# Jobs of a two-layer transformer megakernel laid out anew: layer 0 as a written-out overlapping program, experts' scores from fp16 parts, two plain heads per strip of TensorE, and work moved to ScalarE and GpSimd

## The reference, cut to what matters

```python
x = ln(x + L0_attn(x))   # rms norm; k, v, r = x@W; scan s = ew*s + k*v; (sigmoid(r)*wkv)@Wo;
                         # then rms norm, 128->512 leaky relu, square, 512->128
x = ln(x + L0_ffn(x))    # 8 experts 128->256->128, top 2 of 8, run densely and weighted by the scores
x = ln(x + L1_attn(x))   # "plain" attention: 16 heads of 8, q and k rms-normed per head
x = ln(x + L1_ffn(x))    # 4 experts, each a whole 16-head attention over its own tokens, top 2 of 4
```

## Time and profile before

| | |
|---|---|
| median of 3 runs | 1957.21 us (1956.88 to 1971.77) |
| profiled execution, its own time | 1968.32 us |
| its span, first to last instruction | 1966.5 us |
| busy: TensorE / VectorE / ScalarE / GpSimd | 79% / 56% / 36% / 17% |
| mean granted TensorE clock | 0.828 |
| DMA over the span | 39.13 MB, 20 GB/s |
| layer 0 | about 550 us |
| layer 1 | about 1416 us |

### The profile page before, as it was taken

The page is one execution under the profiler, slowest core; times in us unless marked ns, Lnnn a source line. Parts: engine busy times, 40 slices in busy tenths (PEclk is TensorE's granted clock), DMA queues, the critical chain, the costliest instruction groups (busy, mean ns, idle before and its releaser), DMA issues.

```text
span 1966.5 us, 28835 instructions
## 1 busy us (share of the span) xinstructions
PE 1552.8 (79%) x11376; PEld 899.9 (46%) x11376; DVE 1101.1 (56%) x2692; ACT 705.3 (36%) x1084; POOL 328.0 (17%) x475
## 2 busy tenths in 40 slices
PE   1678877779735778888888888888888888998974
PEld 0455555556512334444454554544545544444533
DVE  1456556565444466566666665656666566546231
ACT  0223323233213234443544434435344353452331
POOL 0000000000031111212222122121220221211111
PEclk9789888898856668889888888898887988988667
DMA  5000000000000000101101101011010110110011
GB/s 164 1 0 0 0 0 0 0 0 0 1 1 12 12 2 13 36 6 35 28 15 36 27 12 30 13 36 27 15 36 6 34 28 15 36 27 16 23 27 29
DMA packets 32417, 39.13 MB, mean 20 GB/s; under 512 B 18004, under 2 KB 25648, under 8 KB 30256
## 3 DMA queue, kind: packets, MB, share of 16 engines
q1 hardware_dynamic: 32304, 37.56, 7.8%
HBM read 33.21 MB, written 2.88 MB: 18 GB/s over the span
## 4 chain that ended last, share of the span: by engine, by line
PE 50%; DVE 12%; issue 4%; ACT 4%; DMA 1%; SPq 1%; POOL 1%; DVEq 0%; POOLq 0%; ACTq 0%
PE ps L1282 47%; DVE mneg_e L1105 3%; DVE q L1168 2%; DVE o_e L1207 1%; ACT k L1042 1%; ACT probs L1005 1%; DVE v_e L1174 1%; PE ps L1445 1%; DVE mneg_l L1105 1%; DVE qkv L1182 1%; PE ps L1395 1%; ACT qT L1075 1%; DVE rqk L1232 1%; PE ps L1451 0%; SPq L871 0%
## 5 line engine op out<-in xcount | busy, mean ns | idle before, releaser
L1005 ACT ACTIVATE probs<-ps 128x1024 f32<-128x1024 f32 x384 | 392.1, 1024 | 401.2 <-PE ps L1282 398.3
L1105 DVE TENSOR_REDUCE mneg_e<-ps 128x2 f32<-128x512 f32 x512 | 341.1, 687 | 244.5 <-PE ps L1282 238.5
L1282 PE MATMUL ps<-q,k 32*128 32x256 f32 x2048 | 309.5, 426 | 10.4 <-DMA q<-shiftT_e 7.9
L1105 DVE TENSOR_REDUCE mneg_l<-ps 128x2 f32<-128x512 f32 x256 | 172.1, 688 | 202.1 <-PE ps L1282 196.7
L1282 PEld LDWEIGHTS ps<-q,k 32*128 32x128 f32 x2048 | 185.9, 199 | 33.1 <-DMA q<-shiftT_e 8.4
L1282 PE MATMUL ps<-probs,v_e 128*32 128x256 f32 x2048 | 173.7, 468 | 16.6 <-DVE qkv L1182 15.4
L1282 PE MATMUL ps<-k,q 32*128 32x256 f16 x1024 | 154.4, 303 | 23.3 <-DVE mneg_e L1105 21.0
L621 PE MATMUL ps<-x3T,w 128*128 128x512 f32 x256 | 147.0, 711 | 0.0
L621 PEld LDWEIGHTS ps<-w,h_moe 128*128 128x128 f32 x1024 | 121.3, 192 | 17.2 <-issue 12.3
L1282 PE MATMUL ps<-x5T,wk 128*128 128x256 f32 x256 | 96.9, 462 | 37.0 <-DVE q L1168 37.0
L621 PE MATMUL ps<-w,h_moe 128*128 128x128 f32 x1024 | 124.2, 276 | 0.0
(11 more groups left out here) (202 smaller groups left out, 2077.1 us busy)
## 6 DMA issues: line engine op xcount, KB each, us to landing
on_e<-scratch_e SPq DMA_DIRECT2D x64, 256.0 KB, 4.5
on_l<-scratch_l SPq DMA_DIRECT2D x64, 128.0 KB, 2.7
sums_e<-o_e SPq DMA_DIRECT2D x128, 4.0 KB, 1.7
out<-y SPq DMA_DIRECT2D x16, 128.0 KB, 1.8
w<-in_w SPq DMA_DIRECT2D x1, 1024.0 KB
qT<-shiftT_l SPq DMA_DIRECT2D x64, 2.0 KB
sums_l<-o_l SPq DMA_DIRECT2D x64, 4.0 KB, 1.7
q<-shiftT_e SPq DMA_DIRECT2D x64, 8.0 KB
```

Of the source, the lines that this page charges most:

```text
L1005: act.activation(probs[:, probs_slot(r, i)].rearrange("p j s -> p (j s)"), s_banks(i).rearrange("p j s -> p (j s)"), ACT.Exp, scale=0.5 if ...
L1105: v.tensor_reduce(to, tiles(max_bank(k)), axis=AX, op=ALU.max, negate=True).then_inc(kind.max_used, 1)
L1282: return pe.matmul(o, l, r, start=start, stop=stop)
```

## The change

1. **Layer 0 written out.** `program_order` lists, for every engine, chunks c = -2 to 8 of 16 steps. In step i TensorE does one half of an expert of chunk c (odd: hidden, even: output) and one piece of the ahead part of chunks c+1 and c+2. No loop, no `meet`, no clearing: semaphores count on over all chunks, and `acc` and `xn` have two buffers. The loads are ordered so that chunk 0 waits only for its own x and four small tensors. The two squares of a chunk that VectorE did on `h_fc` go to ScalarE. The constants of layer 1 and the periods -6 to -4 follow directly, without a block boundary; the wait for the last chunk stands at period -3.
2. **Experts' scores from fp16 parts.** q and k are rounded to fp16 (`q_high`, `k_high`) and the rests (`q_low`, `k_low`) are formed by GpSimd. The scores are high x high + high x low + low x high: 12 fp16 matmuls per E slot in place of 4 fp32 ones. `q32` and `k32` shrink to two block buffers each, which `q_low_ready` and `k_low_ready` free.
3. **Interleaving.** The two `max_scores` of a slot are cut into single matmuls and put between the passes of `scores`; the first of a slot is issued one slot earlier.
4. **Two plain heads per strip.** `v_l` places two heads side by side in a strip of 32, both accumulate in one half of bank 7; `o_l`, `on_l` and their products halve, `wproj` needs 4 matmuls instead of 8, the inverse is fetched by 8 DMAs instead of 4.
5. **The shift of E in two halves** (slots 3 and 8, fp16) instead of one (slot 4): the first half must land before slot 8, the second before slot 16. 
6. **Moved between engines:** evacuation of v (VectorE to ScalarE, its bias folded into `bo` once at the start), both layer norms' last step (to ScalarE), q/k squares (to ScalarE), the Newton steps of the inverse root (to GpSimd, 12 operations).
7. **Moved in time:** the jobs lie in other slots: q at 9, 12, 15, 20, k at 10, 14, 19, 23 (before 5 to 12), routing at 5 and 7 instead of 1 to 3, qT and kT 4 slots apart instead of 1, the output of batch r-2 at slots 2 and 6 instead of r-1 at 16 and 18. Periods run from -6 to 17.

```diff
+        def program_order():
...
+            for c in range(-2, CHUNKS + 1):
+                for i in range(STEPS if c < CHUNKS else LAST_STEPS):
+                    yield True, c, i
+            for r in range(FIRST_PERIOD, B + 2):
+                for i in range(SLOTS):
+                    yield False, r, i
...
+            def hidden_at(c, i):
...
+                k, e = (c + 1, 0) if i == 15 else (c, (i + 1) // 2)
...
+            def output_at(c, i):
...
+                k, e = (c - 1, 7) if i == 0 else (c, i // 2 - 1)
...
+                def round_q(b, g):
+                    if valid(b):
+                        pool.wait_ge(s.q32_ready, G * b + g + 1)
+                        pool.tensor_copy(q_high[:, b % 2, g], q32[:, g % 2]).then_inc(s.q16_ready, 1)
...
+                def rest_of_q(b, g):
+                    if valid(b):
+                        pool.wait_ge(s.q16_ready, G * b + g + 1)
+                        pool.tensor_tensor(q_low[:, b % 2, g], q32[:, g % 2], q_high[:, b % 2, g], ALU.subtract)\
+                            .then_inc(s.q_low_ready, 1)
...
+                def root_steps(b):
...
+                    for n in range(ROOT_STEPS):
+                        link(pool.tensor_tensor(root[:], rqk[:], rqk[:], ALU.mult))
+                        link(pool.tensor_tensor(root[:], root[:], ms[:], ALU.mult))
+                        link(pool.tensor_scalar(root[:], root[:], -0.5, 1.5, ALU.mult, ALU.add))
+                        last = pool.tensor_tensor(rqk[:], rqk[:], root[:], ALU.mult)
...
+                def evacuate_q(b, g):
+                    if valid(b):
                         v.wait_ge(s.q_ps, G * b + g + 1)
                         if g == 0:
                             v.wait_ge(s.pick_ready, b + 1)
+                        if G * b + g > 1:
+                            v.wait_ge(s.q_low_ready, G * b + g - 1)
...
+                def passes(kind, b, g, c, j):
...
+                    return [(k_high[lo:hi, b % 2, g, c, :], q_high[lo:hi, b % 2, g, c, :]),
+                            (k_high[lo:hi, b % 2, g, c, :], q_low[lo:hi, b % 2, g, c, :]),
+                            (k_low[lo:hi, b % 2, g, c, :], q_high[lo:hi, b % 2, g, c, :])]
...
+                    at = (r, i + 1) if i + 1 < SLOTS else (r + 1, 0)
+                    for n in range(3):
+                        scores(*at, 0, n)
+                        if n < T:
+                            max_scores(r, i, 1, n)
+                    for n in range(3):
+                        scores(*at, 1, n)
+                        if n < T:
+                            max_scores(*at, 0, n)
                     weigh(r, i)
                     jobs(r, i)
```

More of the change, by code:

```diff
@@ L495, in _ @@
-            @block.vector
-            def _(v):
-                v.wait_ge(x_loaded, 2 * DMA)
+                    pool.tensor_scalar(var0[:, n, :], src, scale, eps, ALU.mult, ALU.add).then_inc(z.pool_step, 1)
+                    pool.wait_ge(z.pool_step, steps[0])
+                    return pool.tensor_tensor(rstd0[:, n, :], var0[:, n, :], half[:, 0:CT], ALU.pow).then_inc(ready, 1)
+                pool.memset(ident[:], 0.0).then_inc(const_ready, 1)
+                pool.memset(half[:], -0.5)
@@ new lines, in slot @@
+                    k = c - 1 if i == 1 else c
+                    if i % 2 and chunk(k):
+                        e = E0 - 1 if i == 1 else (i - 3) // 2
+                        n = E0 * k + e + 1
+                        v.wait_ge(z.y_ps, n)
+                        if e == 0:
+                            v.wait_ge(z.score_ready, k + 1)
+                        base = x3[:] if e == 0 else acc[:, k % 2]
+                        for t in range(CT):
+                            last = v.scalar_tensor_tensor(acc[:, k % 2, t, :], y_bank[e % 2][:, t * D:(t + 1) * D],
+                                                          score[:, t, e:e + 1], base[:, t, :], ALU.mult, ALU.add)
+                        last.then_inc(z.y_used, 1)
+                        v.wait_ge(z.y_used, n)
@@ L620, in mm, with layer0_tensor @@
+                    if i == 2 and chunk(c - 1):
+                        sums(1, acc[:, (c - 1) % 2]).then_inc(z.acc_sums, 1)
+                return slot
+            def layer0_tensor(pe, take):
                 def mm(o, l, r, start=True, stop=True):
@@ L702, in hidden @@
-                def hidden(e):
-                    if e >= 2:
-                        pe.wait_ge(s.hmoe_ready, e - 1)
-                    for k in range(HB):
-                        last = mm(h_bank[e % 2][:, k, :], w1[:, e, k * P:(k + 1) * P], x3T[:])
-                    last.then_inc(s.hmoe_ps, 1)
-                over_chunks(pe, experts, ahead, meet)
+                        last.then_inc(z.mlp_ps, 1)
+                    if i == 13 and chunk(k):
+                        take(7, z.x3T_ready, k + 1)
+                        pe.wait_ge(z.x3_ready, k + 1)
+                        transposes(x1, x3).then_inc(z.x3T_ps, 1)
@@ L711, in program @@
+                    if i == 8 and chunk(c):
+                        take(7, z.b2_used, c + 1)
+                        pe.wait_ge(z.scoreT_ready, c + 1)
+                        for t in range(CT):
+                            last = mm(x1[:, t * D:(t + 1) * D], scoreT[:, t * P:(t + 1) * P], b2[:])
+                        last.then_inc(z.b2_ps, 1)
+                return slot
         with ExitStack() as ph:
@@ L764, in program @@
             rstd = sb2("rstd_2", [P, 2, T])
+            shift = sb2("shift_2", [P, 2, T])
             lg = sb2("lg_2", [P, T, E1])
@@ L1351, in weigh @@
+                            to = c if kind is E else 0
+                            last = pe.matmul(x1[ROW * j:ROW * (j + 1), to * S:(to + 1) * S], values,
+                                             probs[:, probs_slot(r, first + 2 * t + j // 2), j % 2, c * S:(c + 1) * S],
+                                             start=t == 0 and to == c, stop=t == T - 1 and (kind is E or c == 1),
+                                             skip_group_check=kind is L)
                     if c == 1:
@@ L1466, in slot, with _ @@
                     weigh(r, i)
                     jobs(r, i)
-                schedule(pe, slot)
+                return slot
+            block = ph.enter_context(nc.Block())
+            @block.sync
+            def _(sp):
+                loads(sp)
+                step = attention_sync(sp)
+                for in_layer0, r, i in program_order():
+                    if not in_layer0:
+                        step(r, i)
+                for p in range(2):
+                    sp.wait_ge(y_stored[p], DMA * (B // 2))
@@ new lines, in _, with take @@
+            @block.vector
+            def _(v):
+                layer0, attention = layer0_vector(v), attention_vector(v)
+                for in_layer0, r, i in program_order():
+                    (layer0 if in_layer0 else attention)(r, i)
+            @block.tensor
+            def _(pe):
+                held = {}
+                def take(bank, freed_by, count):
+                    if bank in held:
+                        pe.wait_ge(*held[bank])
+                    held[bank] = (freed_by, count)
+                layer0, attention = layer0_tensor(pe, take), attention_tensor(pe, take)
+                for in_layer0, r, i in program_order():
+                    (layer0 if in_layer0 else attention)(r, i)
```

1522 lines of the change are left out of this document (806 added, 716 removed).

## The result

The changed kernel takes 1554.01 us (median of 4 runs, 1544.68 to 1562.97) where the kernel before took 1964.49 in the same series (1956.88 to 1975.54): a ratio of 0.791, 95% interval 0.784 to 0.797. Predicted were 1607 us, 1500 to 1750. The profiled execution of the changed kernel took 1544.68 us with a span of 1542.9, at a mean granted clock of 0.911 in place of 0.828.

The account below looks back on a forecast made before the run. TensorE was taken as the bound, by its work, idle time and reduced clock. Terms of -18, -105, 0, -5, -194, -25 and -3 sum to -350 us: span 1616, median 1607 us, range 1500 to 1750.

Parts of the forecast that it names:

- rival (a): Whole kernel: all cover holds and the clock stays full, period 59.5 us, pass 44 us, time 1538 us; chance 0.17.
- The start: Start of layer 0: chunk 0 begins at 8 to 12 us instead of 29.67, saving 18 us, bounds 5 to 25.
- Layer 0: Layer 0's seven passes: 46 us each in place of 61, without the meeting and its low clock, saving 105 us.
- The seam: From layer 0's last expert matmuls to the first plain maximum: no saving, 0 us, bounds -8 to +8.
- The filling: From first plain maximum to first shift DMA: one-off latencies, no E scores, -5 us, bounds -30 to +20.
- A period: Layer 1's steady period: 79.2 to 63.6 us by work -6.4, idle time -6.5, clock -2.7; -194 us over 12.4 periods.
- 0.35 us saved, x16 = 5.6 us: Layer 1's E slots: fp16 scores shorten each from 1.07 to 0.72 us at full clock, 5.6 us per period.
- rival (c): Layer 1: GpSimd's list holds back the evacuation of q, period 70 us, time 1697 us; chance 0.13.
- The end: Last periods and end: shorter E slots and no wait for the last shift -25 us, last chain -3 us.
- (b): Layer 1: fp16 scores gain nothing as weight loads are not hidden, period 71.3 us, time 1717 us; chance 0.16.
- (d): Layer 0 does not overlap as meant: VectorE's bursts hold the banks, passes 56 us, time 1677 us; chance 0.10.
- (e): Layer 1: light fp16 passes leave TensorE's clock at 1.2 GHz, slower than before at 2180 us; chance 0.04.

Follow-up runs that it names:

- all_loads_first: The changed kernel with chunk 0's first operation waiting for all of x and all layer 0 weights, as before the change: 1567.5 us, ratio 0.7979.
- run with a drain: The changed kernel with TensorE waiting, per chunk of layer 0, until VectorE has added the last expert's output and taken statistics: 1613.8 us, ratio 0.8215.
- fp32_early: The changed kernel with fp32 expert scores, layer 1's constants set at program start and periods -6 to -4 between steps of layer 0's last chunks: 1524.2 us.
- fp32_scores: The changed kernel with the experts' scores as fp32 matmuls again, without q_low and k_low: 1540.6 us, ratio 0.7843.
- one_pass: The changed kernel with only the high x high pass of the experts' scores, GpSimd still forming the low parts: 1557.7 us, ratio 0.7914.

## Why the prediction was right, and which terms were off

**The total** (span 1616 predicted, 1542.9 measured) was 73 us too long. The median of 1554.0 lies in the range, and below the forecast's own band of 1560 to 1660 (chance 0.40), between it and rival (a) at 1538. Start, filling and end gave more than their terms; layer 0 and the seam came as said; the period came near its number by another way than the sum's.

**The start** (-18, measured -30.1): I put the first operation at 8 to 12 us; it starts at 3.75, and all of that arrives at the first weighted sum. all_loads_first shows that 23 of the 30 us are the loads; no run takes the other 7 apart.

**Layer 0** (46 us per pass, measured 44.9): right, and for the reasons given. Before, 61 us were 48.8 of work at a clock of 0.86 and 12 of idle time; now they are 42.3 at 1.00 and 2.7. The run with a drain shows both causes at work again.

**The seam** (0, measured +3.3): right, inside its bounds. The rows at 405.44 and 406.55 show something not foreseen. VectorE's last four operations of layer 0, 0.34 us each otherwise, took 4.46 us together while GpSimd filled constants, one of them 3.845 us (the largest of the 32, min/median/max in ns):

```profile
L518 DVE TENSOR_SCALAR x_all<-acc,mv,rstd x32: 339/342/3845, 113.5 to 409.5; 128x128 f32<-128x128 f32 x32
```

In fp32_early, whose constants are set at the start of the program, the longest of the same 32 takes 0.742 us. The 3.3 us that the four lost are as much as the miss of this stretch; that the one is the cause of the other was not tried.

**The filling** (-5, measured -25.8, inside the bounds): mis-sized. Its busy time fell from 102.8 to 85.9 us at nearly the same clock (0.61 and 0.66), its idle time from 51.6 to 42.6. I had taken it for latencies alone. The first shift DMA came at 564.67, not at 595. A part of it is the event's own place: only half of the shift leaves there. Measured to the second half, at 574.77, the filling is 138.7 us, 15.7 shorter than before, so 16 to 26 us in all. No run took this stretch apart.

**A period** (63.6 us, measured 62.4 over eleven and 62.1 over the twelve of the table): nearly right as a sum, and wrong in how it is made. Busy time fell by 12.2 us (predicted 9.1). At clocks of 0.87 and 0.94 a period has 21 and 7.5 us at half clock; busy for some nine tenths of it, that is 6 us of the 12, where I had 2.7 of a possible 6 (the 21 us at half clock were there to be read from the 0.87). Idle time fell by 5.6 (predicted 6.5). The other 6 us are less work, and here the step failed that read: 0.35 us saved, x16 = 5.6 us. The slot did shorten (1.07 to 0.76 us, predicted 0.72), but what TensorE saved in it came back as idle time and half clock. With fp32 scores the period is 61.9, and the time 1540.6. I counted the term at its full size on the path without asking, slot by slot, who ends the slot next; VectorE's 1.4 us of maxima per slot stood in my own text. And the eight subtractions that I had called hidden cost 1.7 us per sequence by the ratios; the trace shows VectorE's evacuation of q waiting for them, which is the sign of being wrong that I had named for rival (c). So it is partly luck that the period came out 1.2 us from the forecast: a term of 5.6 us for the scores that no run finds on the path stood in the place of more clock and of gains that I had not counted.

**What made the period short, then**: of 17.7 us, the undoing runs put 5.7 on the interleaved order and 2.1 on VectorE's relief (unclear in time), and they count the fp16 scores as a whole as a loss of 0.5 (within the noise). Such shares need not add up: the order alone, put into the kernel before, gave nothing. About 10 us remain for the new places of the jobs, the second place for v in bank 7, the heads of the maxima, the two plain heads per strip with `wproj`, and for parts that work only together. Of these only kT against qT was tried, at 0. The four waits of the earlier trace rows are gone and so are the stretches at half clock behind two of them, which points to the job places, but that is argued from the trace and not shown by a run.

**The end** (-35, measured -51.5): the period's miss again, over more than three shorter periods.

**The rivals.** (a) is nearest in time, 16 us off, though not as it was meant: the clock is 0.94 in the periods. The run fp32_scores comes closer to it, with eight of eleven periods at 59.9 to 61.4 us and a clock of 1.00. (b) was right in its result and wrong in its reason: the fp16 scores gain nothing, yet the load is hidden. The Trainium skill (TensorE: Matmul & The Clock Gate, Part 3) has, in its list of what overlaps, loads overlap only where the row groups differ; the passes 0.11 us apart in one group don't agree with it, so the measurement decides. The same part also lets a load that targets a background weight buffer run ahead, and with that they do agree. (c) is in the trace, with VectorE waiting 1.6 us for `q_low` in the shown period, a quarter of its price. (d) is out by the passes of 44.9 us. (e) did not come: one_pass, which has the lightest slots, stays at 0.90.

## What to carry to other kernels

Once the busiest engine waits slot by slot for another, work taken from it can turn into gaps, and a TensorE with more gaps ran at a lower clock here (one_pass): ask of each saving which engine ends that slot next, before counting it. Helper work on an engine with room to spare costs what it delays in its own list, so price each moved operation by who waits behind it and not by the engine's total. And test the parts apart: one of the largest parts of this rewrite gave nothing, and the version without it and with the seam overlapped was 2% faster.

## What the runs showed of the hardware

**Which gaps cost the clock.** In slot 4 VectorE takes the reciprocal of sums that a chain of SyncE's DMAs brings; where they come late, its maxima wait, and TensorE for them. The changed kernel at sequence 3, VectorE and then TensorE, and busy times and clock of what followed:

```profile
749.38 0.55 DVE L1302 RECIPROCAL inverse_e<-sums_e 128x64 f32<-128x64 f32 x1 [1.50 <-DMA sums_e<-o_e]
...
751.64 0.58 PE L1367 MATMUL ps<-kT,qT 32*128 32x256 f16 x2 [2.58 <-DVE mneg_e L1191]
...
751.64:761.00 9.36, 9.36 (x63) 5.81 (x64) 3.56 (x8) 1.76 (x3) 1.50 (x2) 0.50 0.08 14
```

Here 2.58 us of gap were followed by 9.4 us at half clock with TensorE fully busy, and the period took 67.7 us. I went through all gaps of TensorE of 0.9 us and more between 620 and 1315 us in the changed kernel and in fp32_scores, 32 in all, with the mean clock of the 3 us and the 6 us behind each. Those of 2.12, 2.58 and 3.01 us were each followed by half clock over all nine microseconds. Of those of 1.79, 1.81, 1.84 and 1.85 us three were followed by a lower clock (0.72 and 0.57, 0.77 and 0.50, 0.74 and 0.84) and one, the longest, by 1.00. Of the other 25 (0.91 to 1.62 us) all but two kept the full clock; those two, of 1.18 and 1.26 us, were followed by 0.50 and 0.53. So the long gaps cost themselves and, with 9.4 us at half clock, some 4 us more (an estimate from the last row), and most gaps of about one microsecond only themselves. The length of the gap alone does not decide it: 1.18 us lost the clock and 1.85 us did not, and no run set the length of a gap with all else equal. A reciprocal a slot or two later might take VectorE off that DMA; it wasn't tried.

**Less work for TensorE came with a lower clock.** Over its four executions one_pass had a mean granted clock of 0.886 to 0.894, the changed kernel 0.898 to 0.911, and fp32_scores, with the most work for TensorE of the three, 0.918 to 0.931. one_pass left out two thirds of the score passes and took as long as the changed kernel (0.7914 against 0.7907).

**Beside GpSimd's long fills an operation of VectorE took 3.845 us in place of 0.34**, and beside GpSimd's two-input operations a two-input product of VectorE took 1.402 us in place of 0.705.
